# Graph network kernel on one Trainium2 core: the first edge pass with weighted one-hots as the loaded operand

## What is computed

```python
h = x @ W
a_s = h @ att_src
a_d = h @ att_dst
e = jax.nn.leaky_relu(a_s[src] + a_d[dst], 0.2)   # a loop edge is added for each node
m = jax.ops.segment_max(e, dst, num_segments=N)
p = jnp.exp(e - m[dst])
denom = jax.ops.segment_sum(p, dst, num_segments=N)
out = jax.ops.segment_sum(h[src] * (p / denom[dst])[:, None], dst, num_segments=N)
```

## Times and profile before

| what | us |
|---|---|
| median of 3 runs | 4463.06 |
| lowest and highest run | 4462.13, 4468.02 |
| span of the profiled execution | 5773.8 |
| of it ahead of the first sums of the first edge pass | 335 |
| of it the first edge pass, first sums to last addition | 1154 |
| of it the rest | 4285 |

### The profile page before, as it was taken

How to read it: one execution, slowest core, us unless ns; L and a number is a source line. 1 busy time by engine, 2 the same in 40 slices (tenths; PEclk the granted TensorE clock), 3 DMA queues, 4 the chain that set the end, 5 groups by cost and what they waited for, 6 DMA issues and landing times. The chain is left out here.

```text
span 5773.8 us, 76309 instructions
## 1 busy us (share of the span) xinstructions
PE 3956.3 (69%) x20694; PEld 3229.1 (56%) x20695; DVE 2133.2 (37%) x6441; ACT 1348.1 (23%) x1886; POOL 2896.8 (50%) x3007
## 2 busy tenths in 40 slices
PE   3755565567667777777777666676767664888888
PEld 1645555557546666666667544454545442666666
DVE  4932222223544333333345532232323343332332
ACT  1000000000221000010005544444444452332322
POOL 3865655563135555555541255555555536555451
PEclk7555555555665555555557866666666665888888
DMA  4521111110232222222211222222222222111111
GB/s 122 175 57 42 43 42 42 42 43 23 79 132 57 54 58 55 55 58 55 55 49 49 83 75 70 72 79 70 77 72 77 70 70 64 37 35 35 34 36 34
DMA packets 256062, 357.37 MB, mean 62 GB/s; under 512 B 52798, under 2 KB 179189, under 8 KB 255861
## 3 DMA queue, kind: packets, MB, share of 16 engines
q0 software_dynamic: 90624, 185.78, 12.2%
q1 hardware_dynamic: 165241, 169.55, 9.9%
HBM read 316.13 MB, written 39.00 MB: 62 GB/s over the span
## 5 line engine op out<-in xcount | busy, mean ns | idle before, releaser
L797 POOL DMA_INDIRECT m_rows<-table,m_idx x1568 | 1506.9, 961 | 1086.2 <-issue 460.9
L797 POOL DMA_INDIRECT m_rows<-table,e_idx x464 | 444.1, 957 | 373.5 <-DVEq L1347 178.9
L797 POOL DMA_INDIRECT m_more<-table,e_idx x480 | 453.4, 945 | 301.3 <-DVEq L1089 162.3
L1110 PE MATMUL e_agg<-e_weights,m_more 128*128 128x16 f32 x1152 | 339.2, 374 | 308.5 <-DMA lo_dram<-su_lob 176.5
L1110 PEld LDWEIGHTS e_agg<-e_weights,m_more 128*128 128x128 f32 x1152 | 311.7, 330 | 334.2 <-issue 334.2
L1111 PE MATMUL e_agg<-e_weights,m_ones 128*128 128x32 f32 x1568 | 481.6, 401 | 1.7 <-issue 1.7
L1435 PE MATMUL e_out<-e_counts,e_nodes 128*128 128x256 bf16 x2964 | 448.9, 307 | 32.4 <-issue 32.3
L1111 PEld LDWEIGHTS e_agg<-e_weights,m_ones 128*128 128x128 f32 x1568 | 428.3, 333 | 0.9 <-issue 0.9
L1548 PE MATMUL e_z<-e_w,e_filt 128*128 128x128 f32 x1568 | 356.3, 396 | 102.5 <-issue 100.4
L1537 PE MATMUL e_z<-e_edge,e_w 128*128 128x512 f32 x392 | 287.5, 871 | 199.3 <-DVEq L1617 168.8
L1548 PEld LDWEIGHTS e_z<-e_w,e_filt 128*128 128x128 f32 x1568 | 311.3, 293 | 180.6 <-issue 180.3
(11 more groups left out here) (304 smaller groups left out, 6332.4 us busy)
## 6 DMA issues: line engine op xcount, KB each, us to landing
e_edge<-edge_T SPq DMA_DIRECT2D x98, 512.0 KB
lu_place<-lo_dram SPq DMA_DIRECT2D x49, 512.0 KB
m_rows<-table,m_idx POOLq DMA_INDIRECT x1568
e_key<-key_dram SPq DMA_DIRECT2D x98, 256.0 KB
key_dram<-key_out SPq DMA_DIRECT2D x13, 1024.0 KB
table<-m_rows SPq DMA_DIRECT2D x39, 256.0 KB, 2.3
m_more<-table,e_idx POOLq DMA_INDIRECT x480
m_rows<-table,e_idx POOLq DMA_INDIRECT x464
```

What stands on the lines that cost most here:

```text
L797: pool.indirect_dma_start(rows[:, t, :], None, table, bass.IndirectOffsetOnAxis(ap=idx[:, t:t + 1], axis=0)).then_inc(landed[q], 16)
L1110: pe.matmul(to[:, 0, cols], s.rows[at.r][:, t, :], both[:, t, 0, :], start=False, stop=False)
```

## The change

- One-hots are 128 columns wide. `place_c` holds each edge's node relative to its chunk's first base, so one window of 128 nodes serves the whole chunk. VectorE builds the one-hot of 8 x 128 columns in one instruction (line 1098), multiplies it by `ad` in the window (line 1100), reduces (line 1101), and makes the weights by one product with p (line 1109). The eight small products are gone.
- TensorE loads the weights (128 edges x 128 nodes) and moves the gathered rows with three added columns behind them: ones, and two that VectorE writes (marked maximum, mark). One matmul of 131 columns a tile (line 1138) in place of two. The result stands by node. ScalarE copies it to SBUF (`take`), TensorE turns it one chunk later by two transposes (lines 1145 and 1146), and VectorE adds two pieces (line 1118).
- A mark is now set on each edge whose value equals its segment's maximum; the number of ties is summed too, and the output phase divides by it (three more instructions there). The third line of the segment phase is gone.
- A slot of the ring is free when its sums are made (`summed`), not when they are added. GpSimd waits for that alone; the pacing is gone. Rows have a pitch of 132, so the ring has 14 slots in the same memory, and 112 tiles are gathered ahead.
- VectorE and ScalarE run two chunks ahead of the additions (`ahead`): weigh(n+2), add(n).

The diff, cut to its core:

```diff
-RING0 = 16
+PITCH = P + 4
+KINDS = 3
...
+                ch.add(v.scalar_tensor_tensor(m.place_c[:], span[:, 1, :], most[:, 0:1], m.place_f[:], ALU.mult, ALU.add))
...
-            pool.wait_ge(s.rows_free[r], turn + 1)
+            pool.wait_ge(s.summed, turn * ring + (r + 1 + RING - ring))
...
-            gather_paced(pool, s.rows[r], s.idx[b][:, r * C:(r + 1) * C], s.gathered[r], table, turn, s.idx_seen,
-                         s.gathered[r - 1] if r else None)
+            gather_chunk(pool, s.rows[r], s.idx[b][:, r * C:(r + 1) * C], s.gathered[r], table)
...
+                def take(at):
+                    act.wait_ge(s.summed, at.n + 1 + RING)
+                    act.wait_ge(turned, at.n + 1)
+                    act.activation(by_node[at.b][:], agg[at.b][:, 0:P + KINDS], ACT.Copy).then_inc(taken, 1)
+
+                def both(now, later):
+                    take(now)
+                    p_of(later)
...
+                for rows in s.rows:
+                    v.memset(rows[:, :, P:P + 1], 1.0).then_inc(cleared, 1)
...
-                        ch = Chain(v, s.chain, n * STEPS)
-                        onehot, ins = onehot_of(v, m, s, chunk, w, b)
-                        ch.step(ins)
-
-                        masked = masked_of[wide].rearrange("p (t w) -> p t w", w=W)
-                        for t, base in enumerate(bases_of(v, nc, k, m.base_i, chunk, w)):
-                            ch.add(v.tensor_tensor(masked[:, t, :], onehot[:, t, :], ad[:, ds(base, W)], ALU.mult))
-                        ch.wait()
-                        ch.step(v.tensor_reduce(ade[:], masked, AX.X, ALU.add))
-
-                        ch.step(v.tensor_tensor(uv[:], m.tl[:, 0:2, ds(chunk * C, C)],
-                                                ade[:].unsqueeze(1).to_broadcast([P, 2, C]), ALU.add))
+                        n, w, b = at.n, at.w, at.b
+                        tiles = ds(at.chunk * C, C)
+                        ch = Chain(v, chain, n * STEPS)
+                        nodes = (m.iota_f if w is None else m.iota_w)[:]
+                        shape = [P, C, CW]
+                        hot = onehot[:].rearrange("p (t w) -> p t w", w=CW)
+                        out = weights[b][:].rearrange("p (t w) -> p t w", w=CW)
+                        ch.step(v.tensor_tensor(hot, nodes.unsqueeze(1).to_broadcast(shape), over(m.place_c[:, tiles], shape), ALU.is_equal))
+                        v.wait_ge(s.summed, n + RING - 1)
+                        ch.step(v.tensor_tensor(out, hot, ad[:, ds(chunk_window(v, k, m, at), CW)].unsqueeze(1).to_broadcast(shape), ALU.mult))
+                        ch.step(v.tensor_reduce(ade[:], out, AX.X, ALU.add))
+                        ch.step(v.tensor_tensor(uv[:], m.tl[:, 0:2, tiles], ade[:].unsqueeze(1).to_broadcast([P, 2, C]), ALU.add))
                         ch.step(v.scalar_tensor_tensor(uv[:], uv[:], SLOPE, uv[:], ALU.mult, ALU.max))
                         v.tensor_tensor(diff[:], uv[:, 0, :], uv[:, 1, :], ALU.subtract).then_inc(diff_ready, 1)
-                        ch.add(v.tensor_copy(pl[b][:, :, 1], m.tl[:, 2, ds(chunk * C, C)]))
+                        first, top = s.rows[at.r][:, :, P + 2], s.rows[at.r][:, :, P + 1]
+                        ch.step(v.tensor_tensor(first, m.tl[:, 0, tiles], m.tl[:, 1, tiles], ALU.is_equal))
+                        ch.add(v.tensor_tensor(top, first, m.tl[:, 1, tiles], ALU.mult))
                         v.wait_ge(p_ready, n + 1)
-                        ch.wait()
-                        both = weights[b].rearrange("p (t kw) -> p t kw", kw=2 * W)
-                        for kind in range(2):
-                            ch.add(v.tensor_tensor(both[:, :, kind * W:(kind + 1) * W], onehot,
-                                                   pl[b][:, :, kind:kind + 1].to_broadcast([P, C, W]), ALU.mult))
+                        ch.add(v.tensor_tensor(out, hot, over(p[b][:], shape), ALU.mult))
                         ch.close(STEPS)
                         v.sem_inc(weights_ready, 1)
...
-                        v.wait_ge(s.agg_ready, at.n + 1)
-                        for n, (window, part) in enumerate(((acc[:, 0, cols], slice(0, P)), (acc[0:HALF, 1, cols], slice(0, HALF)),
-                                                            (acc[HALF:P, 1, cols], slice(HALF, P)))):
-                            v.tensor_tensor(window, window, agg[at.b][part, n * CW:(n + 1) * CW], ALU.add).then_inc(s.added, 1)
-                        v.wait_ge(s.added, 3 * at.n + 3)
-                        v.sem_inc(s.agg_free, 1)
-                        v.sem_inc(s.rows_free[at.r], 1)
-
-                    over_chunks_lagged(v, k, wide, weigh, add, lambda w: next_window(v, m, windows, w), len(s.rows))
+                        v.wait_ge(turned, at.n + 3)
+                        v.wait_ge(added, 2 * at.n + 4)
+                        for window, part in ((acc[:, 0, cols], turn[at.b][:, 0:CW]), (acc[0:KINDS, 1, cols], turn[at.b][0:KINDS, CW:2 * CW])):
+                            v.tensor_tensor(window, window, part, ALU.add).then_inc(added, 1)
+
+                    def both(now, later):
+                        weigh(later)
+                        add(now)
...
                     def sums(at):
-                        rel = tile_windows(pe, nc, k, m, at)
-                        pe.wait_ge(s.agg_free, at.n + 1)
-                        clear_bank(pe, m, agg[at.b], 3 * CW)
+                        pe.wait_ge(taken, at.n + 1)
                         wait_rows(pe, arrived(s, at), at.turn + 1)
                         pe.wait_ge(weights_ready, at.n + 1)
-                        to = agg[at.b][:, 0:3 * CW].rearrange("p (a w) -> p a w", w=CW)
-                        both = weights[at.b].rearrange("p (t a w) -> p t a w", a=2, w=W)
                         for t in range(C):
-                            cols = ds(rel[t], W)
-                            pe.matmul(to[:, 0, cols], s.rows[at.r][:, t, :], both[:, t, 0, :], start=False, stop=False)
-                            ins = pe.matmul(to[:, 1:3, cols], m.ones[:], both[:, t, :, :], start=False, stop=(t == C - 1))
-                        ins.then_inc(s.agg_ready, 1)
-                    over_chunks(pe, k, wide, sums, RING if wide else len(s.rows))
+                            ins = pe.matmul(agg[at.b][:, 0:P + KINDS], weights[at.b][:, t * CW:(t + 1) * CW],
+                                            s.rows[at.r][:, t, 0:P + KINDS], start=(t == 0), stop=(t == C - 1))
+                        ins.then_inc(s.summed, 1)
+
+                    def turn_sums(at):
+                        pe.wait_ge(taken, at.n + 3)
+                        pe.wait_ge(added, 2 * at.n + 2)
+                        pe.transpose(turn[at.b][:, 0:P], by_node[at.b][:, 0:P], m.ident[:])
+                        pe.transpose(turn[at.b][0:KINDS, P:2 * P], by_node[at.b][:, P:P + KINDS], m.ident[:]).then_inc(turned, 1)
+                    over_chunks_lagged(pe, k, wide, sums, turn_sums, lambda w: None, ring)
...
+                ch.step(v.tensor_scalar(ties, ties, 0.5, None, ALU.max))
+                ch.step(v.reciprocal(ties, ties))
+                ch.step(v.tensor_tensor(most, most, ties, ALU.mult))
...
-            early = early_rows(nc, "g0_", [rows[:] for rows in m.rows] + [rows_of(n) for n in range(RING0 - RING)],
+            m.more = sbuf(layer, "more", [P, 3 * RING * C * P])
+            in_rows, in_more = RING * P // PITCH, 3 * RING * P // PITCH
+            rows_in = lambda part, n: part[:, n * C * PITCH:(n + 1) * C * PITCH].rearrange("p (t d) -> p t d", d=PITCH)
+            early = early_rows(nc, "g0_", [rows_in(m.rows_all, n) for n in range(in_rows)] + [rows_in(m.more, n) for n in range(in_more)],
```

162 lines of the change are left out of this document (90 added, 72 removed).

## The result

The changed kernel takes 4669.83 us, the kernel before 4464.39: a ratio of 1.0469, 95% interval 1.0448 to 1.049, or +205 us. The forecast was +161 us and 4620. One of the four executions of the changed kernel, of which there is no trace, took 5239.31 us at a granted clock of 0.523 (0.679 to 0.684 in the others); the ratio leaves it out.

The account below looks back on a forecast made before the run. The prediction took GpSimd to bound the first pass without the crawl: 1178 for start and gathers, 141 for held gathers, 10 and 1 make 1330 against 1169, +161 us on 4463, rounded 4620; range 4460 to 4710.

Parts of the forecast that it names:

- The bound: First edge pass: GpSimd bounds it at 10.0 us a chunk without the crawl; TensorE's saving is worth nothing.
- The crawl: First pass: 1.2 us pauses on VectorE delay slot releases, worth 320 us in the recorded execution, assumed absent from timed ones.
- C: Rival: the crawl is in timed executions and the change removes it, 160 us faster, 4303; chance 0.15.
- A: The forecast itself: first pass GpSimd bound, its gathers lengthened by VectorE, 4530 to 4700 us; chance 0.60.
- D: Rival: VectorE becomes the first pass's bound at 12.5 us a chunk, +70 to +390 us, middle 4690; chance 0.13.
- The hold: First pass: gathers caught in VectorE instructions with two SBUF inputs wait; 294 instructions at 0.48 us, 141 us.
- Rival B: First pass gathers are not held and stay at 945 ns: 0 to +35 us, 4463 to 4498; chance 0.12.
- The start: Start of the first pass: 112 gathers made ahead, GpSimd's ring begins at 338.8 us with 672 gathers left.
- VectorE's chunk: First pass: VectorE's chain takes 8.7 us a chunk, under GpSimd's 10.0 by 1.3.
- Output phase: After the passes: three more operations on 52 columns, about 1 us.

Follow-up runs that it names:

- x2_psum3: The changed kernel with the one-hot and its node numbers in PSUM, so no wide VectorE instruction has both inputs in SBUF: 4478.89 us.
- x7_psum3_ring16: x2_psum3 with a ring of 16 slots in place of 14: 4462.66 us, 0.9991 to the kernel before.
- x5_late_p: The changed kernel with one small extra VectorE reduction per chunk ahead of the product with p: 4616.29 us.
- x6_late_both: x5_late_p with the same small reduction also between the one-hot and its product with ad: 4528.06 us.
- x3_two_in: The kernel before with three extra VectorE additions per chunk, each of two 1024-element SBUF inputs: 4665.45 us, 1.0452.
- x4_one_in: The kernel before with three extra one-input VectorE reductions of 1024 elements per chunk, in the same places as x3_two_in: 4605.99 us, 1.032.
- x1_before: The kernel before, unchanged, recorded again for a trace whose span agrees with its time: 4460.39 us.
- x8_ring14: The kernel before with a ring of 14 slots in place of 16: 4481.04 us, 1.004.
- the long trace: The first recorded execution of the kernel before, on which the prediction was made: 5773.8 us.

## Why the prediction was right, and where its size was off

**The bound.** Right. GpSimd bounds the pass in both kernels; TensorE's saving is worth nothing (x2_psum3, x7_psum3_ring16): its chunk, put at 4.6 us, keeps it busy 4.1 (393.35 us for 96 chunks). The pass of before without the crawl was put at 1169 and ends at 1160.8.

**The crawl.** The assumption that the timed executions do not have it was right, the reason was not. "So the recorded execution carries 1311 us that the timed ones do not have" holds for this one trace, not for recording: after's span agrees with its time to 2 us. The expectation of some 220 us of crawl in the trace of after fell with it, and so did that of a pass of 1100 to 1250 us: from the first sums at 318.9 to the last addition at 1360.0 it takes 1041 us. That is near the 1000 us that were named as the sign of C; the gathers at 1223 ns and the time of before tell C and A apart. Nothing known beforehand said that the timed executions come from chips without the crawl; this much of the forecast was luck, and the chances of C and D stood for it.

**The hold, the term that was mis-sized.** The mechanism and its price for one gather are as read in the earlier trace rows: the end comes 0.81 to 0.85 us behind VectorE's, 0.82 in the median. The mean gather was forecast between 1050 and 1250 ns and is 1223. The step that failed is "for a random phase the loss of one is the area": 0.48 us for each of 294 instructions, 141 us. Measured are 186.6 us, 0.63 each, because the phase is not random. The first held gather puts the next ones 1.12 and 2.37 us behind VectorE's end, and the chain of the chunk starts its products just ahead of those points: line 1098 costs 0.29 each, 1100 0.80 and 1109 0.84. x5_late_p and x6_late_both moved them by 0.4 us and got 54 and 142 us back. That is 46 us more than forecast, where the whole came out 44 above.

The Trainium skill (SBUF — State Buffer, Who interferes with whom) says that a VectorE instruction with two SBUF inputs contends with a GpSimd instruction that reads SBUF, and that one with a single SBUF input (outside two modes that use both ports) or a tensor_reduce does not. With that rule x2_psum3, x3_two_in and x4_one_in agree: 944, 1254 and 947 ns. Its other half, that a probe showed tensor_tensor not stalling DMAs issued from GpSimd, is not what this kernel does: 1.9 us where 0.945 is the rule. Rival B, which rested on it, is out.

**The start.** The first gather of the ring was put at 338.8 and comes at 323.5. Two errors of the step lie in that. The first sums at 335.06 were taken from a chip with the crawl; in x1_before they start at 319.4. And the slot is now free at the sums, where the kernel before waits for the addition as well: sums at 319.44 and first gather at 328.36 before, 318.86 and 323.51 after. The smaller ring costs what was thought (x8_ring14, +17). Since both kernels moved alike, the difference of 13 us (672 x 1.249 from 323.5 against 656 x 1.252 from 328.4) is near the 19 that the prediction had.

**VectorE's chunk.** Put at 8.7, free it is 8.2, and rival D's 12.5 is out. GpSimd's bound held with a margin that was thinner than the 1.3 us a chunk of the text, since the comparison of chunk times leaves out the chunks that lie ready: 804 us of VectorE's work against 840.

**Output phase.** Three more instructions on 52 columns beside GpSimd's work were put at 1 us; with their gaps they take 2.5:

```profile
1375.43 1.28 DVE L2084 TENSOR_SCALAR o_cols<-o_cols 128x52 f32<-128x52 f32 x1
1376.74 0.48 DVE L2085 RECIPROCAL o_cols<-o_cols 128x52 f32<-128x52 f32 x1
1377.26 0.71 DVE L2086 TENSOR_TENSOR o_cols<-o_cols 128x52 f32<-128x52 f32 x1
```

**The sum again.** In the traces, the last gather comes at 1349.98 against 1148.58: +201.4, that is 13 for the start and 186.6 for the hold, and 2 of rounding and copies of indices. Behind it come 2 for the stretch to the second pass, and the third pass is 10 longer (1061 us from first to last gather against 1050), little above what the same code shows from run to run here (1048 to 1059 in x1_before to x4_one_in, x7_psum3_ring16 and x8_ring14). The other stretches are some 6 shorter. Together that is 208 by the spans, and 205 by the medians.

## What to carry to other kernels

An engine that is far from full can still cost time through its operands: where GpSimd issues gathers back to back and is the bound, each long VectorE instruction with both inputs in SBUF costs up to nearly its own length (1.16 us at most here, of 1.21), and one with an input in PSUM cost nothing here. Two engines that meet like this do not meet at random; follow one held instruction to the next before you take a mean. When two engines are compared, multiply each one's chunk by the chunks that it has left, not by the same number.

## What the runs showed of the hardware

- A gather of 128 rows on GpSimd takes 0.945 us and the next starts 0.30 us later. Caught in a VectorE instruction with two SBUF inputs it ends 0.81 to 0.85 us behind that instruction's end, and takes 1.99 us in all in the median of the 86 that the third added instruction of x3_two_in holds, 2.11 at most (1087.74 in x5_late_p). VectorE's instruction is not made longer: 1.225 us with and without. One that starts 0.18 us ahead of the instruction is not held (704.30 in x6_late_both). Nearer to its start there is no sharp line: 12 gathers that start 0.01 to 0.02 us ahead of line 1102's instruction in x6_late_both are not held, three that start 0.07 to 0.08 us ahead of line 1099's in x5_late_p are.
- VectorE's instructions on 1024 elements take 1.21 to 1.23 us with the operands in SBUF or one of them in PSUM.
- Two chips of the same kind ran the same kernel in 4461 and 5678 us. In the slower one VectorE's instructions are as long as ever, and in stretches there are pauses ahead of them, of 1.2 us most often. The Trainium skill (Runtime: NRT & Kernel Launch, Instruction fetch mechanics) names a branch to code outside the fetched window as a cause of stalls. No run here shows it: on another chip the same loop of the same program has 2 such pauses where the long trace has 125.
- TensorE's granted clock in the pass was 0.50, that is 1.2 GHz, in x1_before, where TensorE was busy 711.56 of 822 us, and 0.61 on average in after, where it was busy 393.35 of 1028: between its two levels, so part of the time at 2.4 GHz.
